# One load per expert, another row order in memory, and a bound on the gathers of a routed audio-tower layer

## What is computed

```
h = layer_norm(layer_norm(patches) @ W + b)                 # [448, 512]
h = h + bit_mlp(layernorm(h))                               # ternary weights, inner size 1408
x = layernorm(h)
rw, sel = top_k(softmax(x @ router_w.T), 8)                 # 8 of 32 experts for each token
rw = rw / sum(rw)
for e in range(32):                                         # wg, wu: 512 x 192, wd: 192 x 512
    w_e = sum(where(sel == e, rw, 0))
    acc += (silu(x @ wg[e]) * (x @ wu[e])) @ wd[e] * w_e
return h + acc
```

## Time and profile before

| | us |
|---|---|
| median of 3 runs | 308.67 (306.58 to 308.88) |
| the profiled execution, whole | 307.58 |
| its span, first to last instruction | 305.8 |
| around the span | 1.78 |

### The profile page before, as it was taken

One profiled execution on the slowest core, in us unless ns is written; L12 is line 12 of the kernel. 1 busy time (PEld: TensorE's weight loads), 2 busy tenths in 40 slices (PEclk: granted clock), 3 DMA queues, 4 the chain that ended last, 5 costly groups with the idle time before them and its releaser, 6 DMA issues.

```text
span 305.8 us, 3907 instructions
## 1 busy us (share of the span) xinstructions
PE 279.5 (91%) x1159; PEld 147.4 (48%) x1159; DVE 151.0 (49%) x446; ACT 125.1 (41%) x213; POOL 126.4 (41%) x130
## 2 busy tenths in 40 slices
PE   4899999779999889999999999999989999949991
PEld 1435444455557355655465556555645554533231
DVE  2648999995988523343523333323323322303364
ACT  2347998999974221332133213321322232211101
POOL 4062211976521422246435643464355446443310
PEclk9999999999998699999999999999999999997997
DMA  7999999503998298799999999999999999974883
GB/s 251 332 424 417 381 405 309 189 0 120 336 316 281 52 294 292 259 269 331 341 316 313 352 327 313 323 327 312 310 342 335 301 316 337 324 171 65 162 217 124
DMA packets 27798, 85.51 MB, mean 280 GB/s; under 512 B 4209, under 2 KB 4337, under 8 KB 26785
## 3 DMA queue, kind: packets, MB, share of 16 engines
q1 hardware_dynamic: 19760, 64.78, 61.0%
q0 software_dynamic: 7488, 18.42, 25.2%
q10 hardware_dynamic: 530, 2.08, 2.6%
HBM read 72.34 MB, written 12.92 MB: 279 GB/s over the span
## 4 chain that ended last, share of the span: by engine, by line
PE 39%; DVE 18%; DMA 17%; issue 8%; POOL 4%; ACT 3%; POOLq 0%; DVEq 0%; ACTq 0%
PE ps L1163 17%; DMA scrap<-token_rows,idx 9%; PE ps L1192 7%; DMA sum<-w_t,add_idx 5%; PE ps L1184 4%; PE ps L1195 4%; DMA ring<-sum 3%; DVE big L1443 2%; POOL sum L647 2%; DVE stats L1327 2%; PE ps L1050 2%; DVE raw L1449 2%; PE ps L1217 1%; PE ps L1147 1%; DVE hit L1625 1%
## 5 line engine op out<-in xcount | busy, mean ns | idle before, releaser
L633 POOL DMA_INDIRECT scrap<-token_rows,idx x36 | 35.9, 996 | 83.2 <-DVE idx L1628 46.8
L647 POOL DMA_INDIRECT sum<-w_t,add_idx x32 | 51.3, 1604 | 28.1 <-issue 11.5
L866 ACT ACTIVATE w_t<-ps 128x512 f32<-128x512 f32 x36 | 21.4, 597 | 85.0 <-PE ps L1184 84.8
L1644 DVE COPY w_t<-ps 128x256 f32<-128x256 f32 x34 | 14.4, 425 | 58.8 <-PE ps L1220 45.5
L1639 DVE SCALAR_TENSOR_TENSOR w_t<-ps,scrap,w_t 128x192 f32<-128x192 f32 x32 | 13.2, 413 | 57.1 <-issue 47.3
L871 ACT ACTIVATE w_t<-ps 128x192 f32<-128x192 f32 x34 | 11.2, 330 | 55.9 <-PE ps L1163 50.7
L1163 PE MATMUL ps<-ring,w_t 128*128 128x384 f32 x96 | 33.1, 487 | 0.7 <-ACT w_t L866 0.7
L1184 PE MATMUL ps<-ident,scrap 128*128 128x128 f32 x144 | 24.2, 292 | 10.1 <-DMA scrap<-token_rows,idx 6.6
L555 POOL TENSOR_TENSOR root_out<-root_in,minus_half 112x1 f32<-112x1 f32 x20 | 13.1, 654 | 46.3 <-DVE root_in L1344 46.2
L954 PE MATMUL ps<-raw,last 128*112 128x512 f32 x64 | 31.1, 639 | 0.0
L1163 PE MATMUL ps<-big,w_t 128*128 128x384 f32 x88 | 30.2, 486 | 0.0
(11 more groups left out here) (214 smaller groups left out, 470.6 us busy)
## 6 DMA issues: line engine op xcount, KB each, us to landing
big<-in_ffn_gate_up SPq DMA_DIRECT2D x15, 768.0 KB
ring<-in_ffn_gate_up SPq DMA_DIRECT2D x13, 768.0 KB
raw<-in_ffn_gate_up SPq DMA_DIRECT2D x6, 768.0 KB
last<-in_ffn_gate_up SPq DMA_DIRECT2D x6, 768.0 KB
big<-in_ffn_w_down SPq DMA_DIRECT2D x15, 256.0 KB
ring<-in_ffn_w_down SPq DMA_DIRECT2D x13, 256.0 KB
big<-in_mlp_w_in SPq DMA_DIRECT2D x2, 1536.0 KB, 17.7
big<-in_mlp_w_in SPq DMA_DIRECT2D x2, 1280.0 KB, 20.2
```

The lines of the kernel that those rows point to most:

```text
L633: nc.gpsimd.indirect_dma_start(got[:, got_at(s), :], None, rows_dram[:, :], bass.IndirectOffsetOnAxis(ap=idx[:, s:s + 1], axis=0)).then_in ...
L647: nc.gpsimd.indirect_dma_start(acc_dram[m.two][:, :], bass.IndirectOffsetOnAxis(ap=add_idx[:, m.eight:m.eight + 1], axis=0), y[:, m.four, ...
L866: nc.scalar.activation(x_t[:, m.two, :, :], bank(2 + m.two).rearrange("p (c t) -> p c t", c=4), ACT.Copy).then_inc(xt_ready, 1)
L1644: nc.vector.tensor_copy(h_t[:, m.two, :, :], bank(6)[:, 0:2 * P].rearrange("p (c t) -> p c t", c=2)).then_inc(ht_ready, 1)
```

## The change

Five edits, all of them in one program:

1. The weights of an expert stand in memory as one row of 2560 numbers per partition (gate, up, 128 rows of down, rest). An even expert's load is one transfer of 128 x 10240 bytes, whose last part holds its own rest in partitions 0 to 63 and the rest of the odd expert behind it in partitions 64 to 127. An odd expert's load is one transfer of 128 x 8192 bytes. `down_two` takes both rests from the even slot. The number of bytes for two experts is the same as before.
2. The loads of experts 12 to 31 wait for `y_done` of the tile pair that last used their slots, whole loads at a time. A list's load is two transfers (8192 bytes a partition, and 64 rows of 2048 bytes) behind one wait for `y_done`.
3. Expert 10's load stands ahead of the store of the gate weights and waits for `z_done` alone.
4. The tokens are rows 0 to 447 of the scratch tensors and the spare rows stand behind them. A rank without a token gets row 448 + its partition (an addition in place of the maximum).
5. Gathers from tile 8 on have a bound of 447: a rank with a higher row number moves nothing and keeps what its partition of the buffer held. The first eight, one for each buffer, gather all 128 rows.

```diff
-    def down_loaded(self, u):
-        return 32 * self.k + 32 * ((NE + 4 * self.i + u) // R + 1)
+    def rest_loaded(self):
+        return 16 * self.k + 16
...
+        def pair_rest_of(n):
+            return slots[n - n % 2][rest_rows(n), WG + D:WCOLS]
...
-        rows_v = rows_dram[P:ROWS, :].rearrange("(p g) r -> p g r", g=NG)
-        acc_v = [acc[P:ROWS, :].rearrange("(p g) d -> p g d", g=NG) for acc in acc_dram]
+        rows_v = rows_dram[0:TOK, :].rearrange("(p g) r -> p g r", g=NG)
+        acc_v = [acc[0:TOK, :].rearrange("(p g) d -> p g d", g=NG) for acc in acc_dram]
...
             def load_expert(t):
-                load_gate_up(t, t)
-                load_down(t, t)
+                n, cols = t % R, WCOLS if t % 2 == 0 else WG + D
+                sp.dma_start(slots[n][:, 0:cols], ffn[t, :, 0:cols]).then_inc(ld_gu[n], 16)
+
+            def load_picked(e, n):
+                sp.dma_start(slots[n][:, 0:WG + D], ffn[e, :, 0:WG + D]).then_inc(ld_gu[n], 16)
+                sp.dma_start(down_rest_of(n), ffn[e, 0:IB, WG + D:WCOLS]).then_inc(ld_rest[n], 16)
...
+            sp.wait_ge(z_done, NG)
+            load_expert(10)
             sp.wait_ge(gate_ready, NG)
             sp.dma_start(rows_v[:, :, D:ROW], rows[:, :, D:ROW]).then_inc(rows_out, 16)
-            sp.wait_ge(z_done, NG)
             sp.wait_ge(xt_done, 1)
-            load_expert(10)
             load_expert(11)
             for t in range(R, NE):
-                sp.wait_ge(gu_done, t - R + 1)
-                load_gate_up(t, t % R)
-                sp.wait_ge(y_done, t - R + 1)
-                load_down(t, t % R)
+                sp.wait_ge(y_done, t - R + (1 if t % 2 else 2))
+                load_expert(t)
...
                     e = sp.value_load(owner_row[0:1, bass.ds(NLIST * k + n, 1)], min_val=0, max_val=NE - 1)
-                    sp.wait_ge(gu_done, R * k + (NE - R + n + 1))
-                    load_gate_up(bass.ds(e, 1), s)
                     sp.wait_ge(y_done, R * k + (NE - R + n + 1))
-                    load_down(bass.ds(e, 1), s)
+                    load_picked(bass.ds(e, 1), s)
...
-                                               (token, [[1, NG], [NG, G]], P, 0),
-                                               (iota_p, [[0, 1]], 0, 1), (iota_p2, [[0, 1]], 0, 2)):
+                                               (token, [[1, NG], [NG, G]], -TOK, -1),
+                                               (no_row, [[0, 1]], TOK, 1), (iota_p2, [[0, 1]], 0, 2)):
...
-                nc.gpsimd.indirect_dma_start(got[:, got_at(s), :], None, rows_dram[:, :],
-                                             bass.IndirectOffsetOnAxis(ap=idx[:, s:s + 1], axis=0)
-                                             ).then_inc(ld_got[s], 16)
+                rows_ = bass.IndirectOffsetOnAxis(ap=idx[:, s:s + 1], axis=0)
+                if isinstance(m, Tile) and m.t < 8:
+                    nc.gpsimd.indirect_dma_start(got[:, got_at(s), :], None, rows_dram[:, :], rows_).then_inc(ld_got[s], 16)
+                else:
+                    nc.gpsimd.indirect_dma_start(got[:, got_at(s), :], None, rows_dram[:, :], rows_, bounds_check=TOK - 1,
+                                                 oob_is_err=False).then_inc(ld_got[s], 16)
...
-                nc.vector.tensor_scalar(idx[:, s:s + 1], idx_f[:, s:s + 1], iota_p[:, 0:1], None, ALU.max).then_inc(idx_ready, 1)
+                nc.vector.tensor_scalar(idx[:, s:s + 1], idx_f[:, s:s + 1], no_row[:, 0:1], None, ALU.add).then_inc(idx_ready, 1)
```

More of the change, by code:

```diff
@@ L104, in pairs_of, with program @@
         yield k, n_pairs
-def program(nc, x, w_tok, vecs, gb1, w_in, w_down, g_down, w_router, we_gate_up, we_down, out):
+def program(nc, x, w_tok, vecs, gb1, w_in, w_down, g_down, w_router, ffn, out):
     rows_dram = nc.dram_tensor("token_rows", (ROWS, ROW), F32).ap()
@@ L240, in program @@
         token = sb("token", [128, TOK], F16)
-        iota_p = sb("iota_p", [128, 1], F32)
+        no_row = sb("no_row", [128, 1], F32)
         iota_p2 = sb("iota_p2", [128, 1], F32)
@@ L315, in program @@
         ld_gu = [sem(f"ld_gu{n}") for n in range(R)]
-        ld_dn = [sem(f"ld_dn{n}") for n in range(R)]
+        ld_rest = [sem(f"ld_rest{n}") for n in range(R)]
         ld_got = [sem(f"ld_got{n}") for n in range(8)]
@@ L1189, in down_two @@
                     pe.wait_ge(ht_ready, m.upto())
-                    pe.wait_ge(ld_dn[m.slot], 2 * m.loaded())
                     wait(pe, y_ready, m.upto(-2))
@@ L1194, in down_two @@
                     rows_ = rest_rows(m.slot)
-                    nc.tensor.matmul(bank(4 + m.two), h_t[rows_, m.two, 1, :], down_rest_of(m.slot), start=False, stop=True
+                    nc.tensor.matmul(bank(4 + m.two), h_t[rows_, m.two, 1, :], pair_rest_of(m.slot), start=False, stop=True
                                      ).then_inc(y_done, 1)
@@ L1765, in laid_out @@
     import numpy as np
+    rest = np.zeros((NE, P, D), we_down.dtype)
+    rest[:, 0:IB] = we_down[:, P:IE]
+    rest[0::2, IB:P] = we_down[1::2, P:IE]
     return {
```

16 lines of the change are left out of this document (5 added, 11 removed).

## The result

The changed kernel is slower: 318.35 us median of four runs (317.01 to 320.83), against 307.62 (306.16 to 308.88) for the kernel before, a ratio of 1.036 with a 95% interval of 1.027 to 1.045. The prediction was 299.5 us, with a range of 296 to 309. The sign was wrong, and the time lies outside the range.

A forecast was written before the change was run, and what follows sets the result against it. PE was taken to set the pace, with crowded q0 adding to it. Terms 3.0 + 5.6 + 0.8 - 0.3 = 9.1 us gave 298.5 from the profiled 307.58, 299.6 against the median, stated as 299.5; range 296 to 309.

The forecast's parts named there:

- Fewer, longer rows: Expert weight loads on q1: longer rows raise its rate to 385 GB/s and ease the DMA shortage; 3.0 us gained in ten pairs.
- Later loads: Gate and up loads waiting for `y_done`: they still arrive well before they are needed, so this costs nothing.
- Expert 10 ahead: Expert 10's load before the gate weights' store: delays the store and may touch the first gather; 0.3 us lost.
- Bound and row order: Gathers from tile 8 on: 14% fewer bytes, perhaps 0.1 us of q0 a pair; extra POOL cost taken as 0.
- The end of the tiles: Q1's gather, at the last tiles: lands before it is wanted and the clock stays up; 5.6 us gained.
- The sums: ACT's reading back of the sums: no empty gathers, 1.8 us earlier landing, limited by DVE to 0.8 us gained.
- the pairs before 154 us: Tile pairs ahead of the ten measured ones: may add 1 us of gain, counted only at the good end.
- the slower one: Rival, in the pairs: packet-by-packet turns with long q1 rows starve q0, gathers land 1.0 us late a pair; 317.5 us, chance 0.12.

The follow-up runs named there:

- e3: Changed kernel with its loads cut into transfers of 2048 bytes a row, same bytes and waits: 303.57 us, ratio 0.997 to the kernel before.
- e12: Separate kernel without the computation: one gather or scatter-add, alone or beside weight loads of three row lengths; scatter 4.98 us alone, 10.70 beside 10240-byte rows.
- e10: Changed kernel with loads cut at 8192 bytes, an even expert in 8192 and 2048, an odd one whole: 313.48 us, ratio 1.015.
- e4: Kernel before with only the later loads: gate and up wait for `y_done`, rows of 6144 and 2048 bytes as before: 309.84 us, ratio 1.020.
- e7: Changed kernel with expert 10's load back behind the gate weights' store: 317.79 us, ratio 1.040 to the kernel before.
- e2: Kernel before with only the new row order and the gathers' bound, loads as before: 301.1 us, ratio 0.989.
- e1: Changed kernel without the bound, so all gathers move 128 rows again: 316.57 us, ratio 1.038 to the kernel before.
- e11: Kernel before with row order and bound, plus an odd expert's gate and up load half a pair later: 307.75 us, ratio 1.004.

## Why the prediction was wrong

The failed step is the first term, *Fewer, longer rows*, "I take 3.0". Its own quantities came out near. q1's rate in its share was taken at 385 GB/s and is 362: 23.49 MB in 55.7% of the 116.53 us that the ten pairs take now. The DMA share fell from 1.06 to 0.94. By the step's own reckoning a pair now wants 2.36 / 0.362 = 6.5 us of q1 and 4.4 of q0 (38.0% of the 116.53), 10.9 where it had counted on 10.45: the shortage would have shrunk from 8% to 5%, and 10.9 / 1.06 = 10.3 us is a pair as long as before. Measured are 11.65, and ten pairs that are 13.6 us longer in place of 3.0 shorter. (A share of over 1.00, by which the step counts, does not need two queues: the earlier trace rows have 101.6% with q1 alone.) The step took the pair's length from the DMA engines' whole work, as if it did not matter whose packet goes first. It does matter: POOL's transfers form a chain, scatter behind scatter with the gathers between them, and what counts for the pair is how long one of them takes from issue to landing. Longer rows lengthen exactly that, and leave the engines idle at other times. e3, which cuts the long rows and leaves the rest of the change, has the time back (its ten pairs are 2.9 us shorter than before, with short rows what the term had booked on long ones), and e12 shows the price on a single scatter, 2.3 us. That the turns lengthen the scatters is so shown; that the scatters' chain, and not the gathers by themselves, passes it on to PE is read from the chains of waits of the change and of e10, where scatters of 9.7 to 11.6 us follow each other, and no run changes it alone.

*Later loads*, costed at nothing, was the second failure. The cover that the step named was real: PE waits for no expert's weights in the change or in e4. But it asked only whether the load comes in time, and not what the load runs beside. e4 puts the price at 2.0% when gate and up stay in rows of 6144 bytes. What the change adds by it to a pair's burst is not its size, which is 2.36 MB before as well, but which gate and up stand in it: the pair's own even expert, ahead, in place of the next pair's, last. How that costs 2% is not shown.

*Expert 10 ahead* holds. POOL's timeline of the changed kernel has the first gather 0.2 us later than the earlier trace rows, released by DVE's idx as before, and e7, where it starts at 102.78, finds no difference in the whole:

```profile
103.55 1.21 POOL L634 DMA_INDIRECT scrap<-token_rows,idx  x1 [8.36 <-DVE idx L1629]
```

*Bound and row order* was too small where it was right. q0 moves 1.84 MB less, 1.85 foretold. POOL's cost of a bounded gather is 1.04 to 1.09 us against 0.98 to 1.02 for a plain one, so 0 was nearly right. Alone, bound and row order give 1.1% (e2, 0.7 to 1.6). In e2's trace T(Q0) starts at 267.27 (before 269.15), so 1.9 us are won up to there, 1.4 of them in the ten pairs; T(Q1) follows after 3.26 us instead of 5.10, which is 1.8; and from there to the end it is 28.9 instead of 31.55, 2.7. That is 6.4 us between two single executions; by the ratio it is 3.4. Of the gain that had been booked on long rows in the pairs, the bound brought a part. The rule of the Trainium skill on the swizzle (DMA: Bandwidth & Descriptors, The descriptor swizzle), by which it gains nothing there, is not borne out by these 1.4 us of one profiled execution, and not refuted by them; no run tells the engines apart.

*The end of the tiles*, 5.6, had the right place and most of its size. Between the step's own marks, T(Q0) and ACT's taking of the last product, lay 279.74 - 269.15 = 10.6 us before and lie 290.10 - 283.99 = 6.1 now: 4.5. In the change Q1's gather takes 3.99 us and the wait is 1.68 instead of 4.46; in e2 4.95 and 2.62. It is not the fewer rows that did it: in e1, where Q1's gather moves all 128, it takes 3.98 us and PE waits 0.38, and in e3, with the bound, 7.00 and 3.54. PE's timeline of the changed kernel shows the other part of that step:

```profile
286.30 0.75 PE L1186 MATMUL ps<-ident,scrap 128*128 128x128 f32 x4 [1.68 <-DMA scrap<-token_rows,idx]
...
287.10 1.02 PE L1193 MATMUL ps<-ring,w_t 128*128 128x512 f32 x2
```

Two L1193 take 1.02 us, where the two L1192 of the earlier trace rows took 1.91: the clock stayed up behind the shorter wait, as foretold. (It also did behind the 2.62 us of e2, and fell behind the 2.46 at 247 us, so the length of one wait does not decide it.) *The sums* are read in 8.38 us, 10.45 before, and from ACT's taking of that product to the end it is 25.1 us in place of 26.1: 1.0 where 0.8 was foretold. The 1.8 us that this step set ahead of its limit do not come out of its rows (0.56 of 0.75 MB of 3.25 us is 2.4), which changes nothing, as the 0.8 us of DVE bound it. So the terms of the end, 6.4 together, brought 5.4; the failed ones lie in the pairs, and the pairs before 154 us, which might have added 1, lost 1.1 with all that stands ahead of them.

Of the rivals, the slower one comes out, at 317.5 against 318.35, with a chance of only 0.12. Its parts are only half right. The turns of packet for packet are there, and its price for a q1 packet, 0.31 us of an engine, is what the ten pairs show (0.557 x 116.53 x 16 / 3307 = 0.314). But it let the gathers carry the delay and took the scatters as they were, it did not have the lower clock (4.8 us), and it left Q1's wait as it was. Errors of both signs met near the right sum, so its nearness is in good part luck. The argument that held its chance down was that q1 runs dry once in each pair and q0 then has the engines to itself. The trace has those stretches (197 to 200 us), and they do not help: a scatter alone still takes 5.0 us from issue to landing, and the next but one is issued only when it has landed. A rule of the Trainium skill (DMA: Bandwidth & Descriptors, Queues, rings and completion order) has a round-robin between queues at packet granularity; e12 agrees with 67 against 67 and 30 against 25 packets, in the profile's packets. That page of the Trainium skill, under Rules for kernel authors, advises at least 1 MiB a transfer for the most bandwidth, and one large transfer in place of many small ones; here the same bytes in four or five times as many transfers (e3) stand at 0.997 and the long ones at 1.036, and the measurement decides.

What stays open: why a transfer of POOL gets its first packet 4 us or more after the issue beside a burst, and 2 us after it alone (e12), which may be what the stretches almost without q0 packets are, in the change, before and in e3; why a late load is dear when its rows are of 6144 bytes or less (e4, e11); and what long rows would do with the loads as early as before.

## What to carry to other kernels

When two queues share the DMA engines and one of them carries a chain of short, dependent transfers, count the time of one such transfer from issue to landing, and not only the engines' share: here a DMA share that fell from 1.06 to 0.94 went with a kernel 3.6% slower. Merge transfers only where nothing waits beside them, keep rows of bulk loads at a few KB where something does (2048 and 5120 bytes were alike here, 8192 was not), and ask of a load that is moved what will be issued beside it, not only whether it still arrives in time. Try the parts of a combined change alone: of this one the bound and the row order gave 1.1%, and the other parts hid it. And before a burst or a pause is called the cause, look for it in the kernel that is faster: here both were there before.

## What the runs showed that I had not expected

A rank over the bound still counts as a packet: q0 has 7488 packets with the bound and without it (e1), at 16.58 and 18.42 MB. A gather of 128 rows of 2176 bytes is 80 packets, a scatter-add of 128 rows of 2048 bytes 144. The scatter-add alone takes 5.0 us from issue to landing, the gather 3.5, with fewer bytes in the scatter. And a transfer of POOL that starts beside a burst pays 3.1 to 3.4 us even when the burst's rows are short.
